# One graph layer of a four-layer GNN: neighbour sums placed ahead of the edge weights, a wait for scattered stores moved

## The reference

```python
e_n = leaky(hi[i_idx] + hj[j_idx])                 # leaky: slope 0.05
alpha_n = segment_softmax(e_n, i_idx, N)
x_from_nodes = scatter_mean(alpha_n[:, None] * h[j_idx], i_idx, N)
e_e = leaky(he[i_idx_e] + ge2)
alpha_e = segment_softmax(e_e, i_idx_e, N)
x_from_edges = scatter_mean(alpha_e[:, None] * g2, i_idx_e, N)
```

## Time and profile before

| what | value |
|---|---|
| median of three runs | 3401.27 us |
| profiled execution, first to last instruction | 3409.0 us |
| TensorE / VectorE / ScalarE / GpSimd busy | 52% / 63% / 23% / 46% of the span |
| adjacency loads over the whole program, 1600 KB | 75, median 6.7 us from issue to landing |
| mean granted TensorE clock | 0.804 of full speed |

### The profile page before, as it was taken

How to read it: one execution, slowest core, us unless ns; L and a number is a source line. 1 busy time by engine, 2 the same in 40 slices (tenths; PEclk the granted TensorE clock), 3 DMA queues, 4 the chain that set the end, 5 groups by cost and what they waited for, 6 DMA issues and landing times. The chain is left out here.

```text
span 3409.0 us, 40315 instructions
## 1 busy us (share of the span) xinstructions
PE 1773.6 (52%) x10789; PEld 1203.8 (35%) x10789; DVE 2154.8 (63%) x4340; ACT 779.5 (23%) x1999; POOL 1569.1 (46%) x1514
## 2 busy tenths in 40 slices
PE   4021111131565555438982781288204879984994
PEld 3011111021333333327761561134101238862653
DVE  6654444448666666467768781501767976657986
ACT  2200000012222222212331000100005855532341
POOL 0067777720777777537747577520480005520000
PEclk9999999999766677655555896589557999976997
DMA  7644344453887878879850781075565636624761
GB/s 290 266 109 105 103 106 104 104 34 112 220 242 230 237 232 236 162 89 202 200 132 0 176 183 19 3 271 210 227 255 207 229 122 130 129 56 112 206 187 36
DMA packets 701163, 534.85 MB, mean 157 GB/s; under 512 B 397990, under 2 KB 657638, under 8 KB 686896
## 3 DMA queue, kind: packets, MB, share of 16 engines
q1 hardware_dynamic: 642206, 429.80, 48.9%
q0 software_dynamic: 58752, 102.49, 8.7%
HBM read 371.29 MB, written 160.83 MB: 156 GB/s over the span
## 5 line engine op out<-in xcount | busy, mean ns | idle before, releaser
L652 POOL DMA_INDIRECT table<-pay_own,stage x432 | 424.3, 982 | 456.3 <-ACT q L670 178.5
L973 POOL DMA_INDIRECT adjacency<-gm_slot,slot_tmp x440 | 452.7, 1029 | 220.0 <-issue 132.9
L652 POOL DMA_INDIRECT table<-q,stage x424 | 413.9, 976 | 129.2 <-issue 124.9
L631 PE MATMUL banks<-work,acc 128*128 128x52 bf16 x856 | 98.8, 216 | 619.6 <-DVE acc L618 569.8
L631 PEld LDWEIGHTS banks<-work,acc 128*128 128x128 bf16 x856 | 75.2, 116 | 692.5 <-DVE acc L610 443.0
L713 PE MATMUL banks<-pool,both 128*128 x1320 | 268.7, 378 | 28.6 <-issue 24.4
L2034 POOL TENSOR_TENSOR pool<-pool,raw 128x260 f32<-128x260 f32 x110 | 115.2, 1047 | 353.3 <-DMA pool<-table 243.5
L608 DVE TENSOR_SCALAR acc<-acc,pidx 128x512 bf16<-128x512 bf16 x214 | 81.7, 382 | 267.8 <-DMA acc<-low_rows_by_src 264.0
L610 DVE SCALAR_TENSOR_TENSOR acc<-acc,raw,after 128x128 bf16<-128x128 bf16 x856 | 243.1, 344 | 0.0
L713 PEld LDWEIGHTS banks<-pool,both 128*128 128x128 bf16 x1320 | 164.6, 125 | 102.3 <-issue 44.9
L816 PE MATMUL banks<-q,both 128*128 x1320 | 171.7, 295 | 0.2
(11 more groups left out here) (471 smaller groups left out, 4164.4 us busy)
## 6 DMA issues: line engine op xcount, KB each, us to landing
work<-adjacency SPq DMA_DIRECT2D x75, 1600.0 KB, 6.7
adjacency<-slots SPq DMA_DIRECT2D x30, 1320.0 KB, 32.4
acc<-table SPq DMA_DIRECT2D x110, 332.0 KB
q<-table SPq DMA_DIRECT2D x110, 256.0 KB
pool<-table SPq DMA_DIRECT2D x220, 128.0 KB, 2.4
work<-adjacency SPq DMA_DIRECT2D x25, 832.0 KB, 5.4
work<-adjacency SPq DMA_DIRECT2D x25, 768.0 KB, 5.0
acc<-low_rows_by_dst SPq DMA_DIRECT2D x110, 128.0 KB
```

What stands on the lines that cost most here:

```text
L631: nc.tensor.matmul(to, rohT_keys[k % 2][:, j, :], pairs[o][:, :, bass.ds(n * G + j, 1), :] .rearrange("p h t s -> p h (t s)"), start=True, ...
L652: nc.gpsimd.indirect_dma_start(to, bass.IndirectOffsetOnAxis(ap=stage[k][:, j:j + 1], axis=0), pay[k][:, j, 0:width], None).then_inc(lande ...
L973: nc.gpsimd.indirect_dma_start(adjacency, bass.IndirectOffsetOnAxis(ap=pair_at[:, t:t + 1], axis=0), pair_n[:, t:t + 1], None).then_inc(co ...
```

## The change

GpSimd no longer waits in `neighbour_maxima` for its stores; SP waits for them at the start of `edge_weights`. `edge_weights()` is called after `neighbour_sums()`. The two copied rows are loaded by SP at the start of `neighbour_sums`, ahead of the adjacency loads, in place of SP's wait for them; ScalarE's wait for them stays as it is.

```diff
@@ neighbour_maxima, GpSimd
                             nc.gpsimd.indirect_dma_start(fill_rows[o], bass.IndirectOffsetOnAxis(ap=fill_slot[o][:, b:b + 1], axis=0),
                                                          node_vals[:, b, 2:4], None).then_inc(s_fs, 16)
-                    g.wait_ge(s_fs, 16 * 2 * NB)
@@ edge_weights, SP
                 def _(sp):
+                    sp.wait_ge(s_fs, 16 * 2 * NB)
                     for h, o in enumerate(ORD):
                         sp.dma_start(pairs_t[:, h, :, :].rearrange("r n c -> r (n c)"),
                                      fill_rows[o][0:P * T, :].rearrange("(r n) c -> r (n c)", n=SL)).then_inc(s_ld, 16)
-                    for k, to in enumerate((away2["steep"], away2["flat"])):
-                        sp.dma_start(to, node_rows2[k:k + 1, :].to_broadcast([P, NPAD])).then_inc(s_rl, 16)
                     sp.wait_ge(s_ld, 32)
@@ behind the definition of edge_weights
-        edge_weights()
-
         def neighbour_sums():
@@ neighbour_sums, SP
                 def _(sp):
-                    sp.wait_ge(s_rl, 32)
+                    for k, to in enumerate((away2["steep"], away2["flat"])):
+                        sp.dma_start(to, node_rows2[k:k + 1, :].to_broadcast([P, NPAD])).then_inc(s_rl, 16)
                     for b in range(NB):
@@ behind the definition of neighbour_sums
         neighbour_sums()
+        edge_weights()
```

## The result

Over 15 runs of each, the kernel before has a median of 3400.46 us and the changed one 3407.64 us: 7.2 us slower, ratio 1.0022 with a 95% interval of 1.0014 to 1.0030. That is at the very edge of the 0.2% that a measurement of this kernel was said to tell from no change. The interval, 4.8 to 10.2 us, leaves no doubt of the sign.

What follows compares the result with a forecast made beforehand. Each block was taken to cost its latest engine's time: GpSimd's stores and drain, the edge weights' chain, VectorE in the sums. On 3401.27 us, -4.0 + 9.0 - 1.1 + 0 = +3.9 gave 3405.2 us, range 3402.5 to 3411.3.

Steps and rivals of the forecast that it cites:

- within 0.2%: Whole kernel: the change stays within 0.2%, 6.8 us, of before; chance 0.65, likeliest time 3405.2 us.
- the slower case: Whole kernel: slower by over 0.2%; chance 0.32, from 0.27 for a long drain and 0.05 for a shared queue.
- The wait of GpSimd: End of the maxima: without the wait the drain ends 3.0 us behind the last store, not 6.95; gain 4.0 us.
- The estimate from this block's own drain: End of the maxima: the drain lasts its own 4.14 us, starting right behind the last store; gain 2.8 us.
- The slower rival: End of the maxima: the drain stays 7.0 us or more and hid the wait; +7.9 us, 3409.2 us; chance 0.27.
- The copied rows: Start of the neighbour sums: uncovered rows land at 10.7 us, first product at 15.9, not 6.97; cost 9.0 us.
- The rest of the stage: Neighbour sums behind the first product: later adjacency loads stay covered by VectorE's work, so the pace is kept.
- The loads of the edge weights: Edge weights: without the copied rows on the queue the pairs land sooner; gain 1.1 us, between 0 and 1.3.
- Table load and clock: Neighbour sums: ScalarE's 1.28 us table load lies under the rows' wait; TensorE's clock unchanged at the clearing, 0 ± 1 us.
- the shared queue: Start of the neighbour sums: all five loads finish together, rows land at 15.1 us; +8.3 us, 3409.6 us; chance 0.05.
- a faster kernel by cheap rows: Neighbour sums: rows land in 6.9 us with the shortest drain, -1.5 us, 3399.8 us; faster beyond 0.2% had chance 0.03.
- the signs that were named: Profile after: next block some 3.2 us behind the last store, first product at 15.9 us, first scan without waiting.

Runs made afterwards that it cites:

- e5_rows_alone: The changed kernel with SP waiting for the two copied rows before issuing the first adjacency load of the neighbour sums; one execution, 3406.36 us.
- e3_rows_in_maxima: The changed kernel with the two copied rows loaded at the end of SP's work in the maxima; ratio to the kernel before 0.9994 (0.9985 to 1.0003).
- e7_half_stores: The changed kernel with 24 of GpSimd's 50 stores made in the maxima and 26 left out; one execution, 3384.98 us.
- e4_stores_beside_sums: e3_rows_in_maxima with GpSimd's 50 stores moved from the maxima into the neighbour sums; median 3392.23 us, ratio to the kernel before 0.9945.
- e1_wait_back: The changed kernel with GpSimd's wait for its 50 stores put back at the end of the maxima; ratio to the kernel before 1.0020 (1.0010 to 1.0030).

## Why the prediction was right, and where its terms were off

It held in what bounds the blocks, in the path, and in the range (3402.5 to 3411.3 us, measured 3407.64). The range was wide, +1.2 to +10.0 us, and the single terms kept within the bounds given for them. The predicted 3405.2 us was drawn from the median of the three runs then shown, 3401.27; its difference of +3.9 us was too small by about half, beside 7.2 by the timed runs and 8.3 in the profiles. The case "within 0.2%", 6.8 us, had 0.65. By the medians the result lies 0.4 us beyond it, in the slower case that had 0.32, and the interval, 4.8 to 10.2 us, holds both.

*The wait of GpSimd.* Predicted a gain of 4.0 us, measured 2.0 (6.95 to 4.96), and this is the step that was mis-sized most. I took the middle of seven block ends as if they were draws of one quantity. They are not: the block end of L385 whose 3.0 us I took gives 3.0 us again after the change, and that of L1245 gives 1.5 again, as the sequencers' view shows with the end of their last stores, 2113.67 and 2132.28.

```profile
L385 POOLq DRAIN  x1: 18116/18116/18116, 2098.5 to 2098.5; - x1
L1245 POOLq DRAIN  x1: 11757/11757/11757, 2122.0 to 2122.0; - x1
```

In all ten profiles these two ends measure 2.99 and 1.45 us, while the two long ones among the seven vary, from 6.7 to 8.5 and from 7.6 to 9.0 us. Each block end has a length of its own; that of the maxima is 4.9 to 5.2 us in the five profiles that keep its 50 stores and have no wait in the block, and 7.0 in the two with it. Where the same 50 stores lie beside the neighbour sums, the drain ends 7.3 and 8.1 us behind the last of them, so the length isn't set by the stores alone. The estimate from this block's own drain, started right behind the last store, gave a gain of 2.8 us and was nearer. The slower rival, a drain that stays long, named the direction of the error but did not come true: it asked for 5.9 us or more, and the drain ends at 4.96.

*The copied rows.* Predicted 9.0 us, measured 9.4: the rows landed at 11.2 and not 10.7 us, 0.4 of it by the three loads behind them (`e5_rows_alone`), and the remainder of the chain, 5.2 us, came as worked out. The formula that the prediction quotes from the Trainium skill ("DMA: Bandwidth & Descriptors", section "Anatomy of one DMA") is fitted there on single DMAs of GpSimd's queue, and these two come from SP's; its 9.5 us for the pair is an estimate that lies 1.3 us under the 10.8 measured alone. The run with the rows covered again and the one with half of them show that this term is the cause of the slowdown, and not only a time that agrees.

*The rest of the stage.* Predicted to keep its pace. In the profile of the changed kernel it lost 1.4 us: 0.7 between the first and the last product, and 0.7 in the tail. This is not the cost of the order. From the first product to the next block it takes 188.1 us before, 189.5 in the changed kernel and in three more runs with its order (`e3_rows_in_maxima`, `e7_half_stores`, `e4_stores_beside_sums`), but 187.8 to 188.2 in the other four runs with its order, of which `e1_wait_back` and `e5_rows_alone` differ from the changed kernel by one wait. In both parts the time goes with TensorE's granted clock, as the last section shows.

*The loads of the edge weights.* Predicted a gain of 1.1 us, measured 0.6 in the wait and 0.5 in the block (27.28 to 26.77). I had taken the copied rows behind the pairs as what delayed them. Without them SP still passed its wait 6.5 us behind the first issue (2759.6 - 2753.09), where it had been 7.1. Most of that time is the pairs' own.

*Table load and clock.* The table load lay under the wait, as predicted. The clock was priced at 0 with 1 us to either side, for the clearing of the banks. There it was right: from the setting of the ones to SP's next load it takes 10.3 us before (2795.61 - 2785.32) and 10.5 after (2790.36 - 2779.86). But it moved in other places, the start and the tail of the neighbour sums.

The rivals: the shared queue is refuted, and a faster kernel by cheap rows too. (By its own terms, -4.0 + 13.3 - 1.1, the shared queue's sum was +8.2 and not +8.3.) With the measured terms in their places the sum of the prediction reads -2.0 + 9.4 - 0.5 = +6.9 us, close to the 7.2 of the timed runs; the profile's 8.3 has the 1.4 us of the rest of the stage on top. Of the 3.0 us that the predicted sum lacked, 2.0 are from the drain, 0.6 from the pairs and 0.4 from the rows. Of the signs that were named, two failed: the next block starts 5.2 us behind the last store and not 3.2, and the first scan still waits 0.72 us. None of those that would have refuted the forecast appeared.

## What to carry to other kernels

A block that waits on something else is cover for loads: before a stage is moved, list what was issued in it for the next one, and give those loads a new place that is early enough. Here the reordering cost 9.4 us at the start of the stage, with the rows issued in the block ahead it cost 0.2 there, and its worth lay in a third thing that the change left undone, the 50 stores that could run beside the sums (0.55% faster than before with them there). And where one profile must price a block's end, take the value of this block rather than a middle over others.

## What the runs showed of the hardware that was not expected

GpSimd's DRAIN behind scattered stores takes time even when everything has landed: 4137 ns in both profiles with the wait. Without the wait it ends 4.9 to 5.2 us behind the last store, with 24 stores 6.0 us. Behind the wait it can't be a wait for these stores' landings, and with fewer stores it wasn't shorter; what it does is open.

With TensorE's clock the neighbour sums vary by 1.4 us. In the changed kernel it rose to the level of 2.4 GHz 5.1 us behind the first matmul of the stage, with the wait put back 3.8 us behind it, with the same order of blocks. In the 6 us from the first matmul:

```profile
2565.60:2571.60 6.00, 6.00 (x10) 1.94 (x11) 5.93 (x4) 2.58 (x3) 0.00 (x0) 0.57 0.87 316
```

```profile
2582.70:2588.70 6.00, 6.00 (x11) 1.99 (x12) 5.93 (x4) 3.24 (x3) 0.00 (x0) 0.68 0.84 309
```

The first row is of the changed kernel, the second of the run with the wait put back. ScalarE waits for these matmuls before its seventh exponential of the stage (3.42 us in the changed kernel), and VectorE waits for ScalarE: this is the hold of 1.53 us in the one and 0.88 in the other. In the tail the same 25 transposes took 2.97 us in the changed kernel, at 0.50 granted clock (1.2 GHz), and 1.77 us with the wait put back, at a mean of 0.83 between the two levels:

```profile
2749.00:2753.00 4.00, 2.97 (x25) 2.78 (x25) 2.23 (x4) 0.24 (x1) 0.00 (x0) 0.50 0.00 0
```

```profile
2765.00:2768.70 3.70, 1.77 (x25) 1.64 (x25) 2.04 (x4) 0.67 (x2) 0.00 (x0) 0.83 0.00 0
```

These rows are in the same order as the two above; both tails come behind a pause of over 3 us in which ScalarE copies the sums. In all ten profiles the two go together: a hold of 1.5 to 1.6 us with a tail of 11.7 us from the last product, or a hold of at most 1.2 us with a tail of 10.8 to 10.9. No run moves the clock by itself, so that it is the cause is read from this agreement and not shown. Whatever the cause, kernels with the same order of blocks do with and without these 1.4 us, so they are not the change's own; what is left of the 8.3, 6.9 us, lies close to the 7.2 of the timed runs.
